# First projection stage: the feed-forward product is rounded to 16-bit steps by ScalarE, and its scale moves into the residual addition

## The chip, the cores and the metric

The kernel runs on one core of one Trainium2 chip. The metric is the device time of one execution in microseconds (us), less is better.

## The reference, cut to what matters

The program turns 32 images and texts (NB = 32 samples of T = 273 tokens, D = 256 channels) into tokens, then runs two transformer layers. The part around the change is the end of the first layer's feed-forward block and the entry of the second layer's attention:

```python
def act_qdq(x):                       # 16-bit quantise and dequantise, one scale for the whole tensor
    scale = max(max(abs(x)) / 32767, 1e-12)
    return clip(round(x / scale), -32768, 32767) * scale
o = act_qdq(gate * up)                          # [32, 273, 768]
h = h + o @ lpbq_dequant(w_down).T              # down projection, residual
x = layernorm(h)
q, k, v = split(x @ qkv_w.T)                    # then rotary embedding, norms of some heads
```

## The kernel before

The program is a row of stages, each over all 32 samples. The changed one is `phase_f1`, the first projection stage. It takes about 740 of 5506 us, from 1262 to 2000 us of the trace. For each sample it loads the product `o` (128 partitions x 6 x 273 numbers, f32) and the residual `h`, and does this:

- `round_o` (L1121, ScalarE): `om = o * inv + MAGIC`, which rounds to whole steps in f32.
- `quantise_o` (L1185, VectorE): `o = (om - MAGIC) * scale`, in place.
- `down` (L1277, TensorE): 36 matmuls of 256 columns into PSUM banks 0 and 1.
- `residual` (L1191 and L1193, VectorE): adds PSUM to `h`, in two instructions of 512 and 256 elements. Then come the layer norm's statistics (L98, L102).
- `normalise` (L109, VectorE), `turn_x` (L128, TensorE, transposes), `copy_x` (L1127, ScalarE).
- `project` (L1292 and L1302, TensorE): 12 matmuls of 512 columns for queries and keys into banks 4 to 6, 12 of 256 for the values. `values_and_squares` (L1132, L1135, L1145, ScalarE) copies the values out.
- `rotate` (L1214 to L1228, VectorE), `norms` (L1150, ScalarE), `scale_heads` (L1233 to L1240, VectorE).
- `turn_heads` (L1320, TensorE): turns queries and keys through banks 2, 3 and 1. `upper_parts` (L1157, L1166, ScalarE) and `lower_parts` (L1249, L1258, VectorE) split each turned tile into three bf16 parts, which SP stores.

Everything has two buffers (`u` = sample number modulo 2). Each engine runs its functions in a fixed order, written out by hand: `pipeline` calls, in each turn b, every listed function for sample b plus its lead. Semaphores order the engines; an instruction that waits holds back all that stand behind it on its engine. The orders before are

```python
pipeline(act, NB, ((copy_x, 0), (round_o, 2), (upper_parts, -1), (values_and_squares, 0), (norms, 0)))
pipeline(dve, NB, ((scale_heads, -1), (quantise_o, 2), (residual, 1), (lower_parts, -1), (normalise, 1),
                   (rotate, 0)))
pipeline(pe, NB, ((turn_x, 0), (down, 1), (turn_heads, -1), (project, 0)))
```

So VectorE does `scale_heads` of sample b-1, then `quantise_o` of sample b+2, then `residual` of sample b+1. `down` of b+1 is followed on TensorE by `turn_heads` of b-1, which waits for that residual, because bank 1 holds both the last third of the down product and a turned tile:

```python
if not isinstance(n[0], int) or 2 * n[0] + n[1] + 2 < NB:
    pe.wait_ge(S["h2"].sem, S["h2"].at((n[0], n[1] + 2)))
```

Of the kernel before, what the change touches and what calls it, by code (L numbers as in the profile page):

```python
# [7 lines left out]
ALU = mybir.AluOpType  # L8
ACT = mybir.ActivationFunctionType
AX = mybir.AxisListType  # L10

D = 256
CT = D // 128
PATCHES, TEXT = 196, 77
T = T_BATCH = PATCHES + TEXT
R = 91
NT = T // R
# [3 lines left out]
FT = FF // 128  # L21
# [5 lines left out]
MAGIC = 12582912.0  # L27
# [28 lines left out]
def signals(ctx, nc, prefix, **pers):  # L56
    return {k: Signal(nc, f"{prefix}_{k}", per, skew) for skew, (k, per) in enumerate(pers.items())}
# [80 lines left out]
def phase_a(nc, c, ps, NB, patches_dram, txt_dram, wtok_dram, wq_dram, wk_dram, wv_dram, wo_dram,  # L138
# [4 lines left out]
    with ctx:  # L143
# [3 lines left out]
        def sem(name):  # L147
            return nc.alloc_semaphore("a_" + name)
# [30 lines left out]
        passed = sem("passed")  # L179
        S = signals(ctx, nc, "a", tok=1, tok_out=1, bn=NT + 1, mv=1, eps=1, rstd=1, xn=NT, xT=1, xT_out=1,  # L180
                    g=1, g_out=1, v=1, v_out=1, s=NT, mx=NT, nb=1, p=NT, pT=1, pT_out=1, rden=1, y=1, h1=1,
# [15 lines left out]
        def _(sp):  # L197
# [7 lines left out]
            def next_patches(n, u, i):  # L205
                if following(n, NB):
                    sp.wait_ge(S["tok"].sem, S["tok"].at(n))
                    sp.sem_inc(passed, 1)
                    load_patches((n[0], n[1] + 2), u)

            def store_h1(n, u, i):
                sp.wait_ge(S["h1"].sem, S["h1"].at(n))
                sp.sem_inc(passed, 1)
# [6 lines left out]
            def store_x0(n, u, i):  # L220
                sp.wait_ge(S["x0T_out"].sem, S["x0T_out"].at(n))
                sp.sem_inc(passed, 1)
                sp.dma_start(x0_dram[batch_of(n)].rearrange("(c p) t -> p c t", p=128), x0T[:, u])\
                    .then_inc(x0_stored[u], 16)
# [15 lines left out]
        def _(pool):  # L240
            for k in ("eps", "rstd", "eps1", "rstd1"):
                S[k].give(pool)

            def deviation_h(n, u, i):
                ln_rstd(nc, pool, c, mv[:, u], var_eps[:, u], rstd[:, u], S["mv"], S["eps"], S["rstd"], n)

# [345 lines left out]
def back(n, by):  # L592

    return (n[0], n[1] - by)
# [353 lines left out]
def pipeline(eng, NB, stages):  # L948

    def turn(i, b):
        for stage, lead in stages:
            k = b + lead
            if not isinstance(i, int) or 0 <= 2 * i + k < NB:
                stage((i, k), k % 2, i + k // 2)

    for b in range(-3, 2):
        turn(0, b)
    with eng.Fori(1, NB // 2 - 2) as i:  # L960
        for b in range(2):
            turn(i, b)
    for b in range(5 + NB % 2):
        turn(NB // 2 - 2, b)
# [7 lines left out]
def following(n, NB):  # L972

    return not isinstance(n[0], int) or 2 * n[0] + n[1] + 2 < NB
# [7 lines left out]
def phase_f1(nc, c, ps, NB, magic, o_dram, h1_dram, downT, scale, inv, wqkv_dram, curv_dram,  # L982
# [3 lines left out]
    ctx = ExitStack()  # L986
    with ctx:
        def sb(name, shape, dt=F32):
            return ctx.enter_context(nc.sbuf_tensor("f_" + name, shape, dt))

        def sem(name):
            return nc.alloc_semaphore("f_" + name)
# [8 lines left out]
        wqkv = sb("wqkv", [128, CT, 3 * D])  # L1001
        icurv = sb("icurv", [R, 4])
        o = sb("o", [128, 2, FT, T])
        om = sb("om", [128, 2, FT, T])
        h = sb("h", [R, 2, NT, D])
        stats = sb("stats", [R, 2, NT, 6])
        mv = sb("mv", [R, 2, NT, 2])
        var_eps = sb("var_eps", [R, 2, NT])
        rstd = sb("rstd", [R, 2, NT])
        xn = sb("xn", [R, 2, NT, D])  # L1010
        xT = sb("xT", [128, 2, CT, T])
        rc = sb("rc", [R, 2, 2, HD, H])
# [3 lines left out]
        sq = sb("sq", [R, 2, 2, HD, NSCALED])  # L1016
        ss = sb("ss", [R, 2, NT * 2, NSCALED])
        norm = sb("norm", [R, 2, NT * 2, NSCALED])
        parts = sb("parts", [128, 2, NTILE, PARTS, T], BF16)
        rest = sb("rest", [128, 2, 2, T])  # L1020
# [6 lines left out]
        h_stored = [sem(f"h_stored{u}") for u in range(2)]  # L1027
        p_stored = [sem(f"p_stored{u}") for u in range(2)]
        v_stored = [sem(f"v_stored{u}") for u in range(2)]
        S = signals(ctx, nc, "f", om=1, oq=1, y=1, h2=1, bn=NT + 1, mv=1, eps=1, rstd=1, xn=NT, xT=1, xT_out=1,  # L1030
                    qk=NT, v=2, v_out=2, rc=2 * NT, rot=NT, sq=NT, ss=NT, cap=2, norm=1, inv=1, tq=2, scaled=NT,
                    turn=NTILE, hi=NTILE, rest=NTILE, mid=NTILE, lo=NTILE)
        block = ctx.enter_context(nc.Block())
# [78 lines left out]

        @block.scalar
        def _(act):
            for k in ("om", "xT_out", "v_out", "sq", "norm", "hi", "mid"):
                S[k].give(act)

            def round_o(n, u, i):
                act.wait_ge(o_loaded[u], 16 * (i + 1))
                act.wait_ge(S["oq"].sem, S["oq"].before(n))  # L1120
                nc.scalar.activation(om[:, u], o[:, u], ACT.Identity, scale=inv, bias=magic)\  # L1121
                    .then_inc(S["om"].sem, 1)

            def copy_x(n, u, i):
                act.wait_ge(S["xT"].sem, S["xT"].at(n))
                act.wait_ge(S["v"].sem, S["v"].before(n))
                nc.scalar.copy(xT[:, u], ps[:, 2:4, 0:T]).then_inc(S["xT_out"].sem, 1)  # L1127

            def values_and_squares(n, u, i):
                act.wait_ge(v_stored[u], 16 * i)  # L1130
                act.wait_ge(S["v"].sem, S["v"].at(n, 1))
                nc.scalar.copy(vp[:, u, 0:2, :, 0:HD], ps[0:R, 7, :].rearrange("p (t h w) -> p t h w", t=2, w=HD))\  # L1132
                    .then_inc(S["v_out"].sem, 1)
                act.wait_ge(S["v"].sem, S["v"].at(n, 2))
                nc.scalar.copy(vp[:, u, 2, :, 0:HD], ps[0:R, 0, 0:D].rearrange("p (h w) -> p h w", w=HD))\  # L1135
                    .then_inc(S["v_out"].sem, 1)
                for t in range(NT):
                    act.wait_ge(S["rot"].sem, S["rot"].at(n, t + 1))

                    if t:  # L1140
                        act.wait_ge(S["ss"].sem, S["ss"].at(n, t))
                    else:
                        act.wait_ge(S["ss"].sem, S["ss"].before(n))
                    heads = qk[:, u, t, :, :, 6:16]
                    nc.scalar.activation(sq[:, u], heads, ACT.Square).then_inc(S["sq"].sem, 1)  # L1145

            def norms(n, u, i):
                act.wait_ge(S["cap"].sem, S["cap"].at(n))
                act.wait_ge(S["scaled"].sem, S["scaled"].before(n))
                nc.scalar.activation(norm[:, u], ss[:, u], ACT.Sqrt).then_inc(S["norm"].sem, 1)  # L1150

            def upper_parts(n, u, i):
                act.wait_ge(p_stored[u], STORES * i)
                for j in range(NTILE):
                    rows = ROWS[j]
                    act.wait_ge(S["turn"].sem, S["turn"].at(n, j + 1))
                    nc.scalar.copy(parts[0:rows, u, j, part_place(TILES[j][0], 0), :],  # L1157
                                   ps[0:rows, TURN[j % 3], 0:T]).then_inc(S["hi"].sem, 1)
                    if j:
                        second_part(n, u, j - 1)  # L1160
                second_part(n, u, NTILE - 1)

            def second_part(n, u, j):
                rows = ROWS[j]
                act.wait_ge(S["rest"].sem, S["rest"].at(n, j + 1))
                nc.scalar.copy(parts[0:rows, u, j, 1, :], rest[0:rows, u, j % 2]).then_inc(S["mid"].sem, 1)  # L1166

            pipeline(act, NB, ((copy_x, 0), (round_o, 2), (upper_parts, -1), (values_and_squares, 0), (norms, 0)))

        @block.vector  # L1170
        def _(dve):
            for k in ("oq", "h2", "bn", "mv", "xn", "rc", "rot", "ss", "inv", "tq", "scaled", "rest", "lo"):
                S[k].give(dve)
            dve.wait_ge(w_loaded, 32)
            nc.vector.reciprocal(icurv[:], icurv[:]).then_inc(filled, 1)
# [4 lines left out]
            nc.vector.memset(vp[:], 1.0).then_inc(filled, 1)  # L1180
            dve.wait_ge(filled, 3)

            def quantise_o(n, u, i):
                dve.wait_ge(S["om"].sem, S["om"].at(n))
                nc.vector.tensor_scalar(o[:, u], om[:, u], MAGIC, scale, ALU.subtract, ALU.mult)\  # L1185
                    .then_inc(S["oq"].sem, 1)

            def residual(n, u, i):
                dve.wait_ge(S["y"].sem, S["y"].at(n))
                dve.wait_ge(h_loaded[u], 16 * (i + 1))  # L1190
                nc.vector.tensor_tensor(h[:, u, 0:2, :], ps[0:R, 0, :].rearrange("p (t d) -> p t d", t=2),  # L1191
                                        h[:, u, 0:2, :], ALU.add)
                nc.vector.tensor_tensor(h[:, u, 2, :], ps[0:R, 1, 0:D], h[:, u, 2, :], ALU.add)\  # L1193
                    .then_inc(S["h2"].sem, 1)
                dve.wait_ge(S["h2"].sem, S["h2"].at(n))
                dve.wait_ge(S["xn"].sem, S["xn"].before(n))
                ln_stats(nc, dve, h[:, u], stats[:, u], mv[:, u], (S["bn"].sem, S["bn"].at(n)), S["mv"])
# [57 lines left out]
            def third_part(n, u, j):  # L1255
# [2 lines left out]
                nc.vector.tensor_tensor(parts[0:rows, u, j, part_place(TILES[j][0], 2), :], rest[0:rows, u, j % 2],  # L1258
                                        parts[0:rows, u, j, 1, :], ALU.subtract).then_inc(S["lo"].sem, 1)

            pipeline(dve, NB, ((scale_heads, -1), (quantise_o, 2), (residual, 1), (lower_parts, -1), (normalise, 1),
                               (rotate, 0)))

        @block.tensor
# [1266 lines left out]
```

## Time and profile before

| | |
|---|---|
| median of 3 runs | 5524.6 us (5519.47 to 5539.08) |
| profiled execution | 5507.82 us, its span 5506.1 us |
| TensorE busy | 4410.9 us (80%) |
| VectorE busy | 3717.9 us (68%) |
| ScalarE busy | 2374.3 us (43%) |
| GpSimd busy | 599.8 us (11%) |
| mean granted TensorE clock | 0.867 of full speed |

The span is the time from the first to the last instruction on the core. Shares of busy time are means over stages with different limits, so they do not say what bounds the changed stage. PE is TensorE, PEld its weight load, DVE VectorE, ACT ScalarE, POOL GpSimd, SPq the queue of SyncE. In the rows below a timeline row gives start, length, engine, line and operation, output and inputs, count, and in brackets the idle time of the engine ahead of it with what ended it. A row of the windows view gives the stretch and its length, then the busy time of PE, PEld, DVE, ACT and POOL with the number of instructions, then the granted TensorE clock, the share of the DMA engines and GB/s. A row of the groups view gives line, engine, operation, names, shapes and count, then the busy time in us, the mean ns of one, and the idle time before them.

### The profile page before, as it was taken

What the parts mean: (1) busy time and instruction counts of PE and PEld (TensorE: products, weight loads), DVE (VectorE), ACT (ScalarE), POOL (GpSimd) and SP (SyncE); (2) the same over time, 40 slices, a digit from 0 to 9 for tenths busy, and PEclk for the clock granted to TensorE, in tenths of its full rate; (3) what the DMA queues carried; (4) which work ended last, traced back from release to release, by engine and by line L of the source; (5) the groups of instructions that cost most, each with busy time, mean ns of one, the idle gap of its engine ahead of it and who ended that gap; (6) DMA issues with size and microseconds to landing.
All of it is one profiled execution on the core that took longest, in us unless ns stands there. A gap on an engine that the chain in (4) does not pass through costs nothing. (4 is left out here: it accounts for less than half of the span.)

```text
span 5506.1 us, 99275 instructions
## 1 busy us (share of the span) xinstructions
PE 4410.9 (80%) x26575; PEld 2865.4 (52%) x26575; DVE 3717.9 (68%) x9205; ACT 2374.3 (43%) x5474; POOL 599.8 (11%) x928
## 2 busy tenths in 40 slices
PE   6999788506888857777777767776998999688898
PEld 5777666303555535555555545554555555344444
DVE  4555439766777867766666645556777777477776
ACT  1222237552333337677767732223666666100000
POOL 0111000000000010000000011111111111122221
PEclk8999999857999977777777778888999999899999
DMA  2222369994444432222222235554333333211110
GB/s 80 76 73 76 125 232 385 372 418 146 129 123 129 131 81 69 69 75 71 66 69 75 69 86 155 155 156 105 93 92 92 92 89 75 68 52 46 49 46 26
DMA packets 389665, 635.48 MB, mean 115 GB/s; under 512 B 44598, under 2 KB 311412, under 8 KB 389492
## 3 DMA queue, kind: packets, MB, share of 16 engines
q1 hardware_dynamic: 377172, 632.25, 37.9%
q0 software_dynamic: 12320, 1.40, 0.2%
q8 instruction: 50, 0.82, 0.1%
q14 instruction: 123, 1.01, 0.1%
HBM read 353.96 MB, written 278.15 MB: 115 GB/s over the span
## 5 line engine op out<-in xcount | busy, mean ns | idle before, releaser
L1729 DVE TENSOR_REDUCE e_neg<-ps 91x1 f32<-91x273 f32 x1536 | 571.9, 427 | 136.2 <-PE ps L1550 128.8
L1662 ACT ACTIVATE e_probT<-ps 91x273 f32<-91x273 f32 x1536 | 491.5, 392 | 290.2 <-PE ps L1550 289.6
L2404 PE MATMUL ps<-m_we,m_xT 128*128 128x512 f32 x1104 | 524.2, 624 | 0.0
L1277 PE MATMUL ps<-k_downT,f_o 128*91 128x256 f32 x1152 | 260.1, 385 | 230.3 <-DVE f_o L1185 230.2
L1548 PE MATMUL ps<-c_mask_kq,c_identb 91*91 91x91 bf16 x1536 | 325.9, 243 | 110.7 <-ACT g_probT L1662 81.1
L1550 PE MATMUL ps<-e_k,e_q 96*91 96x273 bf16 x1536 | 343.5, 305 | 62.1 <-DMA e_k<-s_parts 27.3
L2338 DVE SCALAR_TENSOR_TENSOR m_acc<-ps,m_weight,m_acc 128x256 f32<-128x256 f32 x552 | 261.8, 481 | 178.9 <-PE ps L2404 168.4
L1550 PE MATMUL ps<-g_q,g_k 102*91 102x273 bf16 (+5 forms) x1536 | 329.4, 295 | 49.7 <-DVEq L1735 48.2
L1277 PEld LDWEIGHTS ps<-k_downT,f_o 128*91 128x91 f32 x1152 | 182.9, 161 | 299.1 <-issue 231.3
L2404 PEld LDWEIGHTS ps<-m_we,m_xT 128*128 128x128 f32 x1104 | 212.5, 199 | 224.7 <-issue 212.2
L1550 PE MATMUL ps<-e_q,e_k 128*91 128x273 bf16 x1536 | 285.6, 290 | 38.5 <-DMA e_q<-e_shift 36.6
L1548 PEld LDWEIGHTS ps<-c_mask_kq,c_identb 91*91 91x91 bf16 x1536 | 217.8, 152 | 182.5 <-ACT g_probT L1662 139.1
L1550 PEld LDWEIGHTS ps<-e_k,e_q 96*91 96x91 bf16 x1536 | 173.6, 123 | 246.8 <-DVE e_neg L1729 194.6
L1662 ACT ACTIVATE g_probT<-ps 91x273 f32<-91x273 f32 x768 | 263.7, 388 | 51.4 <-PE ps L1550 47.4
L1548 PE MATMUL ps<-c_mask_qk,c_identb 91*91 91x91 bf16 x960 | 216.5, 252 | 79.2 <-DVE g_neg L1729 39.6
L1619 PE MATMUL ps<-g_probT,g_vp 128*32 128x273 f32 (+2 forms) x3072 | 256.2, 415 | 23.9 <-ACT g_probT L1662 23.9
L1619 PE MATMUL ps<-e_probT,e_vp 128*32 128x273 f32 x3072 | 258.9, 409 | 8.8 <-ACT e_probT L1662 6.1
L1550 PEld LDWEIGHTS ps<-g_q,g_k 102*91 102x91 bf16 (+1 forms) x1536 | 219.2, 151 | 86.7 <-DVEq L1735 80.7
L1533 POOL DMA_DIRECT2D e_q<-e_shift x288 | 144.5, 508 | 767.4 <-DVE e_shift L1771 761.5
L1550 PEld LDWEIGHTS ps<-e_q,e_k 128*91 128x91 bf16 x1536 | 176.0, 124 | 96.5 <-issue 37.2
L606 PE MATMUL ps<-c_x,k_upT 128*128 128x273 f32 x768 | 186.9, 400 | 47.1 <-DMA c_x<-s_xq 47.1
L1550 PE MATMUL ps<-g_k,g_q 102*91 102x273 bf16 (+2 forms) x960 | 221.1, 302 | 0.0
(306 smaller groups left out, 9435.6 us busy)
## 6 DMA issues: line engine op xcount, KB each, us to landing
s_gate<-b_gate SPq DMA_DIRECT2D x32, 819.0 KB
c_g<-s_gate SPq DMA_DIRECT2D x32, 819.0 KB, 11.7
s_up<-c_up SPq DMA_DIRECT2D x32, 819.0 KB
s_gated<-c_gated SPq DMA_DIRECT2D x32, 819.0 KB
d_g<-s_gated SPq DMA_DIRECT2D x32, 819.0 KB, 10.0
d_u<-s_up SPq DMA_DIRECT2D x32, 819.0 KB, 10.3
s_o<-d_o SPq DMA_DIRECT2D x32, 819.0 KB
f_o<-s_o SPq DMA_DIRECT2D x32, 819.0 KB, 4.6
```

The lines of the kernel that those rows point to most:

```text
L606: last = nc.tensor.matmul(ps[:, f, 0:T], w[:, k, f * 128:(f + 1) * 128], x[:, k, :], start=(k == 0), stop=(k == CT - 1))
L1277: last = nc.tensor.matmul(ps[0:R, t // 2, (t % 2) * D:(t % 2 + 1) * D], o[:, u, k, t * R:(t + 1) * R], downT[:, k, :], start=(k == 0), sto ...
L1533: pool.dma_start(q[rows + part:rows + part + 1, u, lo:hi, :], shift[0:hi - lo, u, part, :]).then_inc(laid[u], 16)
L1548: nc.tensor.matmul(ps[0:R, bank, col + col_of_mask:col + col_of_mask + R], c["identb"][0:R, 0:R], c[mask][0:R, 0:R], start=True, stop=Fals ...
L1550: return nc.tensor.matmul(out_, stationary, moving, start=mask is None, stop=True, skip_group_check=mask is not None)
L1619: last = nc.tensor.matmul(ps[32 * a:32 * a + VW, 6, q0:T], vp[:, u, kt, ORDER[j], :], probT[:, j % 8, b, col:col + T - q0], start=(kt == 0 ...
L1662: nc.scalar.activation(probT[0:R, p % 8, b, :], src, ACT.Exp, scale=float(HD) ** 0.5 if kinds[h] == COS else 1.0)\
L1729: last = nc.vector.tensor_reduce(neg[:, u, t, h:h + 1], src, AX.X, ALU.max, negate=True)
L2338: nc.vector.scalar_tensor_tensor(out=acc[:, u, t], in0=ps[0:R, EBANK[m % 4], j * D:(j + 1) * D], scalar=weight[:, u, t, 2 * p + j:2 * p + ...
L2404: last = nc.tensor.matmul(ps[0:R, EBANK[m % 4], :], xT[:, u, k, t * R:(t + 1) * R], we[:, k, 2 * p:2 * p + 2, :].rearrange("p e d -> p (e ...
```

## The change

ScalarE's rounding pass writes whole steps as int16 into a new buffer `steps` (the conversion rounds) in place of `om`. A second ScalarE pass, `restore_o`, behind `upper_parts`, copies the steps back into `o` as f32, without the scale. VectorE's `quantise_o` is gone. The down projection so yields the product divided by `scale`, and `residual` multiplies by `scale` while it adds (`scalar_tensor_tensor` with a per-partition scalar in place of `tensor_tensor`).

```diff
-        om = sb("om", [128, 2, FT, T])
+        steps = sb("steps", [128, 2, FT, T], mybir.dt.int16)
...
             def round_o(n, u, i):
                 act.wait_ge(o_loaded[u], 16 * (i + 1))
-                act.wait_ge(S["oq"].sem, S["oq"].before(n))
-                nc.scalar.activation(om[:, u], o[:, u], ACT.Identity, scale=inv, bias=magic)\
-                    .then_inc(S["om"].sem, 1)
+                act.wait_ge(S["oq"].sem, S["oq"].at(back(n, 2)))
+                nc.scalar.activation(steps[:, u], o[:, u], ACT.Identity, scale=inv).then_inc(S["steps"].sem, 1)
+
+            def restore_o(n, u, i):
+                act.wait_ge(S["steps"].sem, S["steps"].at(n))
+                nc.scalar.copy(o[:, u], steps[:, u]).then_inc(S["oq"].sem, 1)
...
-            pipeline(act, NB, ((copy_x, 0), (round_o, 2), (upper_parts, -1), (values_and_squares, 0), (norms, 0)))
+            pipeline(act, NB, ((copy_x, 0), (round_o, 2), (upper_parts, -1), (restore_o, 2), (values_and_squares, 0), (norms, 0)))
...
-            def quantise_o(n, u, i):
-                dve.wait_ge(S["om"].sem, S["om"].at(n))
-                nc.vector.tensor_scalar(o[:, u], om[:, u], MAGIC, scale, ALU.subtract, ALU.mult)\
-                    .then_inc(S["oq"].sem, 1)
-
             def residual(n, u, i):
...
-                nc.vector.tensor_tensor(h[:, u, 0:2, :], ps[0:R, 0, :].rearrange("p (t d) -> p t d", t=2),
-                                        h[:, u, 0:2, :], ALU.add)
-                nc.vector.tensor_tensor(h[:, u, 2, :], ps[0:R, 1, 0:D], h[:, u, 2, :], ALU.add)\
+                nc.vector.scalar_tensor_tensor(out=h[:, u, 0:2, :], in0=ps[0:R, 0, :].rearrange("p (t d) -> p t d", t=2),
+                                               scalar=scale[0:R], in1=h[:, u, 0:2, :], op0=ALU.mult, op1=ALU.add)
+                nc.vector.scalar_tensor_tensor(out=h[:, u, 2, :], in0=ps[0:R, 1, 0:D], scalar=scale[0:R],
+                                               in1=h[:, u, 2, :], op0=ALU.mult, op1=ALU.add)\
                     .then_inc(S["h2"].sem, 1)
...
-            pipeline(dve, NB, ((scale_heads, -1), (quantise_o, 2), (residual, 1), (lower_parts, -1), (normalise, 1),
+            pipeline(dve, NB, ((scale_heads, -1), (residual, 1), (lower_parts, -1), (normalise, 1),
                                (rotate, 0)))
```

## Rows read from the trace of the kernel before

**Rows 1.** Windows view: 27 samples together, then four samples one after another.
```profile
1320.98:1918.81 597.83, 534.01 (x2187) 325.33 (x2188) 479.33 (x1162) 223.83 (x486) 42.39 (x108) 0.90 0.44 126
1608.77:1630.10 21.33, 17.88 (x81) 11.17 (x82) 17.66 (x43) 8.21 (x18) 1.57 (x4) 1.00 0.50 148
1630.10:1652.57 22.47, 20.90 (x82) 12.76 (x82) 17.84 (x43) 8.41 (x18) 1.57 (x4) 0.85 0.38 111
1652.57:1675.74 23.17, 20.90 (x81) 12.35 (x81) 17.83 (x43) 8.21 (x18) 1.57 (x4) 0.85 0.45 122
1675.74:1697.52 21.78, 19.51 (x82) 11.88 (x82) 17.72 (x43) 8.31 (x18) 1.57 (x4) 0.92 0.43 130
```
**Rows 2.** Windows view: the start of the second of these samples.
```profile
1630.20:1636.90 6.70, 6.34 (x20) 3.54 (x21) 6.17 (x19) 3.63 (x10) 1.07 (x2) 0.50 0.69 216
```
**Rows 3.** Timeline from the down projection to the turned heads that follow it.
```profile
1619.72 8.01 PE L1277 MATMUL ps<-k_downT,f_o 128*91 128x256 f32 x36
...
1626.26 1.75 ACT L1121 ACTIVATE f_om<-f_o,k_magic,k_inv_o 128x1638 f32<-128x1638 f32 x1
1626.29 0.89 DVE L1240 TENSOR_TENSOR f_qk<-f_qk,f_norm 91x192 f32<-91x192 f32 x3
...
1628.05 1.07 DVE L1185 TENSOR_SCALAR f_o<-f_om,k_scale_o 128x1638 f32<-128x1638 f32 x1 [0.87 <-ACT f_om L1121]
1629.03 0.68 DVE L1191 TENSOR_TENSOR f_h<-ps,f_h 91x512 f32<-91x512 f32 x1
...
1630.10 1.63 PE L1320 MATMUL ps<-c_ident,f_qk 91*128 91x91 f32 x9 [2.38 <-DVE f_h L1193]
...
1633.05 7.25 PE L1292 MATMUL ps<-f_wqkv,f_xT 128*91 128x512 f32 x12
```
**Rows 4.** Timeline, the same place one sample earlier.
```profile
1608.77 0.93 PE L1320 MATMUL ps<-c_ident,f_qk 91*128 91x91 f32 x9 [1.21 <-DVE f_h L1193]
...
1611.35 5.32 PE L1292 MATMUL ps<-f_wqkv,f_xT 128*91 128x512 f32 x12
```
**Rows 5.** Timeline, the same place one sample later.
```profile
1650.31 1.07 DVE L1185 TENSOR_SCALAR f_o<-f_om,k_scale_o 128x1638 f32<-128x1638 f32 x1 [1.19 <-ACT f_om L1121]
...
1652.57 0.92 PE L1320 MATMUL ps<-c_ident,f_qk 91*128 91x91 f32 x9 [1.21 <-DVE f_h L1193]
```
**Rows 6.** ScalarE around the new pass: timeline, then its wait over the 27 samples.
```profile
1613.80 0.42 ACT L1166 CAST f_parts<-f_rest 8x273 bf16<-8x273 f32 x1 [0.39 <-DVE f_rest L1249]
...
1618.43 0.58 ACT L1132 COPY f_vp<-ps 91x512 f32<-91x512 f32 x1 [4.21 <-PE ps L1302]
...
  PE ps L1302: 159.2, 27
```
**Rows 7.** Groups view by form, ScalarE.
```profile
L1121 ACT ACTIVATE f_om<-f_o,k_magic,k_inv_o 128x1638 f32<-128x1638 f32 x32 | 56.1, 1754 | 24.1 <-DMA f_o<-s_o 24.1
...
L791 ACT ACTIVATE c_sig<-c_steps,k_scale_gate 128x1638 f32<-128x1638 int16 x32 | 53.2, 1664 | 0.0
...
L904 ACT ACTIVATE d_gs<-d_g,k_inv_gated 128x1638 int16<-128x1638 f32 x32 | 53.1, 1660 | 89.7 <-DMA d_g<-s_gated 47.8 <-DVE d_o L920 41.9
...
L1127 ACT COPY f_xT<-ps 128x546 f32<-128x546 f32 x32 | 19.5, 610 | 16.3 <-PE ps L128 13.6 <-issue 2.8
```
**Rows 8.** Groups view by form, VectorE.
```profile
L351 DVE SCALAR_TENSOR_TENSOR a_h<-ps,a_rden,a_h 98x256 f32<-98x256 f32 x64 | 28.0, 480 | 97.4 <-PE ps L467 97.4
...
L1191 DVE TENSOR_TENSOR f_h<-ps,f_h 91x512 f32<-91x512 f32 x32 | 21.9, 685 | 16.1 <-PE ps L1277 15.3
...
L1193 DVE TENSOR_TENSOR f_h<-ps,f_h 91x256 f32<-91x256 f32 x32 | 13.1, 410 | 0.0
```
**Rows 9.** Timeline, the stage's first samples.
```profile
1275.10 9.68 PE L1277 MATMUL ps<-k_downT,f_o 128*91 128x256 f32 x36 [230.21 <-DVE f_o L1185]
...
1317.09 0.89 DVE L1240 TENSOR_TENSOR f_qk<-f_qk,f_norm 91x192 f32<-91x192 f32 x3
...
1319.83 0.68 DVE L1191 TENSOR_TENSOR f_h<-ps,f_h 91x512 f32<-91x512 f32 x1
```

More of the change, by code:

```diff
@@ L1029, in phase_f1 @@
         v_stored = [sem(f"v_stored{u}") for u in range(2)]
-        S = signals(ctx, nc, "f", om=1, oq=1, y=1, h2=1, bn=NT + 1, mv=1, eps=1, rstd=1, xn=NT, xT=1, xT_out=1,
+        S = signals(ctx, nc, "f", steps=1, oq=1, y=1, h2=1, bn=NT + 1, mv=1, eps=1, rstd=1, xn=NT, xT=1, xT_out=1,
                     qk=NT, v=2, v_out=2, rc=2 * NT, rot=NT, sq=NT, ss=NT, cap=2, norm=1, inv=1, tq=2, scaled=NT,
@@ L1114, in _ @@
         def _(act):
-            for k in ("om", "xT_out", "v_out", "sq", "norm", "hi", "mid"):
+            for k in ("steps", "oq", "xT_out", "v_out", "sq", "norm", "hi", "mid"):
                 S[k].give(act)
@@ L1166, in second_part @@
                 nc.scalar.copy(parts[0:rows, u, j, 1, :], rest[0:rows, u, j % 2]).then_inc(S["mid"].sem, 1)
-            pipeline(act, NB, ((copy_x, 0), (round_o, 2), (upper_parts, -1), (values_and_squares, 0), (norms, 0)))
+            pipeline(act, NB, ((copy_x, 0), (round_o, 2), (upper_parts, -1), (restore_o, 2), (values_and_squares, 0), (norms, 0)))
         @block.vector
         def _(dve):
-            for k in ("oq", "h2", "bn", "mv", "xn", "rc", "rot", "ss", "inv", "tq", "scaled", "rest", "lo"):
+            for k in ("h2", "bn", "mv", "xn", "rc", "rot", "ss", "inv", "tq", "scaled", "rest", "lo"):
                 S[k].give(dve)
```

## The prediction

> **What bounds the stage.** I read the windows view first, cut at the instants at which TensorE starts the turned heads. The stage goes in a steady step: 27 samples take 597.83 us, 22.14 each [rows 1]. TensorE is busy for 534 of them and VectorE for 479, so neither is full, and the question is which wait ends last. The four single samples differ: 21.33, 22.47, 23.17 and 21.78 us, 22.19 on average, and their granted clock differs with them: 1.00, 0.85, 0.85, 0.92. I call them A, B, C and D; the mean over 27 samples says that this group of four stands for the loop.
>
> The timeline shows the two things that lengthen them. First a gap on TensorE. The down projection ends at 1619.72 + 8.01 = 1627.73, and the turned heads behind it start at 1630.10, 2.38 us later, released by the residual [rows 3]. One sample earlier and one later the same gap is 1.21 us [rows 4, 5]. The reader is to see why: VectorE has finished the head scaling at 1626.29 + 0.89 = 1627.18, before the down projection ends, but the next thing in its order is the quantise pass, which waits for ScalarE's rounding (1626.26 + 1.75 = 1628.01) and ends at about 1629.1. Only then does the residual start, at 1629.03. In [rows 5] the quantise pass starts at 1650.31 and is over just as the down projection ends, so there it delays nothing. So one gap in four is 1.17 us too long, and in the other three the residual itself is the 1.21 us.
>
> Second, the clock. After the long gap the granted clock is 0.50, that is 1.2 in place of 2.4 GHz, over 6.70 us [rows 2], and the 12 projection matmuls take 7.25 us [rows 3] against 5.32 at full clock [rows 4]. What the engine did before it fell: it stood idle for 2.38 us. But C and D have low stretches too, and ahead of these stood gaps of only 1.21 us, as ahead of A, which has none. So a gap of 1.21 us is enough at some places and not at others.
>
> Without a fall and without a late residual a sample takes 21.33 - 1.17 = 20.16 us (A less the excess of the gap at its end). Measured against that, the clock costs 0 in A, 22.47 - 20.16 = 2.31 in B, 3.01 in C and 1.62 in D: 1.73 a sample on average. The excess gap is 0.29 a sample. 20.16 + 0.29 + 1.73 = 22.18, which closes against [rows 1].
>
> **The change, part by part.**
>
> *VectorE loses the quantise pass*: 32 x 1.07 us [rows 3], and the residual loses the wait for ScalarE that stood in its way. The head scaling is over 0.55 us before the down projection ends, so in an A the residual will start when TensorE releases it. Every gap then is the short one: -0.29 us a sample. Next late behind the residual is the residual itself, which nothing in this change shortens.
>
> *The residual's two instructions become multiply-and-add* with a scalar read from each partition. The nearest row, with PSUM, scalar and SBUF operand in the same places, takes 480 ns for 256 elements, and the addition of 256 that it replaces takes 410 [rows 8]. I charge 0.07 us once for this and 0.06 for the 512-element one (685 now): +0.13 us a sample. It lies on the path, in the gap. Bounds: 0, if the extra time is hidden in the overlap of two neighbours, and 0.14, both in full.
>
> *ScalarE's rounding pass* loses the bias and writes int16. The nearest row with just these operands is 1660 ns against 1754 now [rows 7]: 0.09 us less. It stands between 1626.26 and 1628.01 and the turned heads, the next to need ScalarE, come after, so I count nothing.
>
> *ScalarE gains the restoring pass*, int16 to f32, 1638 elements. The trace does not have a plain copy of that size. Its nearest row, an activation from int16 to f32 of the same shape, takes 1.66 us; three copies of 546 elements would be 1.83 as an upper bound, and VectorE's pass of 1.07 a lower one [rows 3, 7]. I take 1.66. What hides it: ScalarE ends the casts at 1613.80 + 0.42 = 1614.22 and idles 4.21 us for the value matmuls, and over 27 samples that wait adds up to 159.2 us, 5.9 each [rows 6]. 1614.22 + 1.66 = 1615.9 leaves 2.5 us in a sample at full clock. The values' copy, the squares and the norms stand behind it on ScalarE, and TensorE's next down projection behind the values' copy. If the cover were gone, all 1.66 would be on the path. The down projection needs the restored `o` one turn later, at 1619.72, 3.8 us after it is ready. No DMA is added or moved, and the load of the next `o` still waits for the down projection alone, so SP's queue keeps its order.
>
> A rule speaks against this part. The Trainium skill, "ScalarE: Activation LUTs", section "Rules for kernel authors", says to give plain adds and multiplications to VectorE and not to ScalarE, since VectorE is the faster one there. The rows agree on the price (1.66 against 1.07 us), and by that rule the move would add about 0.6 us to each of 32 samples, some 19 us, where the work was not hidden; here the idle stretch of ScalarE decides. The same page, "What ACT_TABLE_LOAD costs", gives 186 ns + 0.833 ns an element for an activation with constant scale and bias; my estimate from it is 1.55 us for the restoring pass, which would leave the sum as it is.
>
> *The clock.* This is the large term and the trace of before does not hold it: every gap will be 1.21 + 0.13 = 1.34 us and none 2.38. Bounds: at best the clock holds in all samples, as in A (0). At worst each sample loses what C loses (3.01). Between them I look at the samples that had the short gap ahead: A, C and D lose 0, 3.01 and 1.62, on average 1.54. But C and D always come one and two samples after the long gap of B, and an A comes as soon as that is past, so I take the long gap as what throws the rhythm off, and falls as rarer without it. They will not vanish, since a gap of 1.21 us has been seen to be enough. I take half of that average, 0.77 us a sample. This is a choice and no row proves it.
>
> *The start.* The first down projection waits for the quantised `o` with nothing to cover it [rows 9]: 1.66 in place of 1.07, +0.59 us once. The first residual in the loop starts at 1319.83, though the head scaling was over at 1317.98 and the down projection earlier: -1.85 once. Together -1.3.
>
> **Sum.** A sample: 20.16 + 0.13 + 0.77 = 21.06 us, in place of 22.14: -1.08. 27 of them make -29.2, the start -1.3: -30.5 us. The profiled execution (5507.8 us, 1.7 of it outside the span) would go to 5477. It was faster than all three runs shown; from their median of 5524.6 the same step gives 5494 us, 0.55% less.
>
> **Rivals.**
> - *The clock holds throughout.* A sample of 20.29 us: 27 x 1.85 + 1.3 = 51 us less, 5473. For it: A. Against it: C and D.
> - *The clock falls as before.* Its loss stays between 1.54 and 1.73: 27 x 0.31 + 1.3 = 9.7, or 27 x 0.12 + 1.3 = 4.5 us less: 5515 to 5520. For it: two of three short gaps now are followed by a fall.
> - *The clock falls in each sample* (slower). The place is the gap ahead of the turned heads, now of one length and so perhaps locked to the clock's rhythm at a bad spot. The price is C's: 20.29 + 3.01 = 23.30, 27 x 1.16 - 1.3 = 30 us more, 5555. It decides from a mean loss of 1.90 us. For it: C. Against it: two C never stand side by side.
> - *ScalarE becomes the late one.* The restoring pass sits in front of the values' copy; it decides once the casts end 2.5 us later than now. At full price 27 x (1.66 - 1.08) - 1.3 = 14 us more, 5539. Against it: 5.9 us of mean idle time.
>
> **How the numbers follow.** Only about 0.5%, 27.6 us, can be told from no change. My forecast gets 0.60, with a range of its own from 5487 to 5501 (a clock loss of 0.5 to 1.0 us a sample); a good two thirds of it, 0.43, lie beyond 0.5%. The holding clock gets 0.12, all faster; the old clock 0.17, all same; the bad lock 0.06, of which 0.05 slower; late ScalarE 0.05, of which 0.01 slower. Faster 0.55, same 0.39, slower 0.06. The range goes from the holding clock to the old one, 5472 to 5520, and leaves out the two slower cases and the ends.
>
> **What would show it right or wrong.** Right: no gap near 2.4 us ahead of the turned heads, all at 1.3; a residual pair longer by 0.13 us; the two ScalarE passes near 1.66 us each, and 2.5 us or more still idle ahead of the values' copy; the loop near 21.1 us a sample, its granted clock up from 0.90 to about 0.95. Wrong: gaps that are gone while the clock stays at 0.90 (the old clock), a clock near 0.85 in every sample (the bad lock), or TensorE's down projection waiting for ScalarE.

## The result and the profile after

The changed kernel takes 5494.56 us (median of 6 runs, 5478.89 to 5510.71) where the kernel before, timed beside it, takes 5530.7. The ratio is 0.9936, 95% interval 0.991 to 0.9961: 0.64% faster. The forecast was 5494 us and 0.55%. The profiled execution took 5478.89 us with a span of 5477.2; against the profiled execution before, the span is 28.9 us shorter, where the sum had said 30.5.

The windows view of the changed kernel, first 27 samples from turned heads to turned heads, then four single samples, then 23 samples that start behind the first three. It answers to [rows 1].

```profile
1324.52:1897.03 572.51, 508.42 (x2188) 312.21 (x2188) 453.91 (x1135) 259.94 (x513) 42.43 (x108) 0.95 0.46 133
1604.09:1624.37 20.28, 17.89 (x82) 11.17 (x82) 16.79 (x42) 9.58 (x19) 1.58 (x4) 1.00 0.45 139
1624.37:1644.64 20.27, 17.87 (x81) 11.16 (x81) 16.79 (x42) 9.67 (x19) 1.57 (x4) 1.00 0.49 140
1685.19:1708.45 23.26, 20.86 (x81) 12.31 (x82) 16.87 (x42) 9.57 (x19) 1.57 (x4) 0.85 0.40 122
1708.45:1730.34 21.89, 19.49 (x82) 11.91 (x82) 16.80 (x42) 9.67 (x19) 1.57 (x4) 0.92 0.43 129
1392.36:1876.74 484.38, 429.24 (x1863) 264.23 (x1864) 386.54 (x966) 221.29 (x437) 36.15 (x92) 0.96 0.46 134
```

The loop goes from 22.14 to 572.51 / 27 = 21.20 us a sample and its granted clock from 0.90 to 0.95. A sample without a fall of the clock is 20.28 us; C and D of before are still there (23.26 and 21.89), but now they come as a pair after three or four samples at full clock, and B with its long gap is gone. In all, 11 of the 27 samples hold a fall, against 20 before.

The timeline of one sample, from VectorE's head scaling to the turned heads and on to the values' copy, answers to [rows 3, 4, 6]:

```profile
1621.57 1.66 ACT L1121 ACTIVATE f_steps<-f_o,k_inv_o 128x1638 int16<-128x1638 f32 x1
1621.60 0.89 DVE L1239 TENSOR_TENSOR f_qk<-f_qk,f_norm 91x192 f32<-91x192 f32 x3
1623.17 0.75 DVE L1189 SCALAR_TENSOR_TENSOR f_h<-ps,k_scale_o,f_h 91x512 f32<-91x512 f32 x1 [0.69 <-PE ps L1276]
...
1624.37 0.92 PE L1319 MATMUL ps<-c_ident,f_qk 91*128 91x91 f32 x9 [1.33 <-DVE f_h L1191]
...
1626.35 0.45 PE L1319 MATMUL ps<-c_ident,f_qk 91*128 91x91 f32 x3 [1.06 <-DVE f_rest L1248]
...
1629.71 1.55 ACT L1125 CAST f_o<-f_steps 128x1638 f32<-128x1638 int16 x1
```

The residual now waits for TensorE (0.69 us of idle VectorE in front of it) and not for ScalarE's rounding. The gap ahead of the turned heads is 1.33 us here, and 1.33 or 1.34 in every sample of the loop but the first (1.97); before, one gap in four was 2.37 or 2.38.

Where the low clock sets in shows in the sample of 23.26 us, and likewise in C of before (the last row):

```profile
1685.19 0.92 PE L1319 MATMUL ps<-c_ident,f_qk 91*128 91x91 f32 x9 [1.34 <-DVE f_h L1191]
1687.19 0.72 PE L1319 MATMUL ps<-c_ident,f_qk 91*128 91x91 f32 x3 [1.07 <-DVE f_rest L1248]
...
1654.56 0.71 PE L1320 MATMUL ps<-c_ident,f_qk 91*128 91x91 f32 x3 [1.07 <-DVE f_rest L1249]
```

The first nine turned matmuls still run as fast as at full clock (0.92 us). The next three, behind TensorE's second wait, of 1.07 us, take 0.72 us where they take 0.45 at full clock. So two idle times stand close together ahead of such a fall, and the prediction names only the first.

The groups view, of the stage, answers to [rows 7, 8]:

```profile
L1121 ACT ACTIVATE f_steps<-f_o,k_inv_o 128x1638 int16<-128x1638 f32 x32 | 53.2, 1662 | 22.3 <-DMA f_o<-s_o 22.3
L1125 ACT CAST f_o<-f_steps 128x1638 f32<-128x1638 int16 x32 | 49.7, 1552 | 0.1
...
L1189 DVE SCALAR_TENSOR_TENSOR f_h<-ps,k_scale_o,f_h 91x512 f32<-91x512 f32 x32 | 23.9, 747 | 61.1 <-PE ps L1276 61.0
L1191 DVE SCALAR_TENSOR_TENSOR f_h<-ps,k_scale_o,f_h 91x256 f32<-91x256 f32 x32 | 15.1, 471 | 0.0
```

### The profile page after: what moved, and what is told of

Its sections match the earlier page's. It is cut to its first block and busy times, and to the rows that moved or that the text cites. A ratio compares the mean times of both kernels' runs of the same rounds, so it can differ in the third digit from the quotient of the medians.

```text
span 5477.2 us, 99287 instructions
## 1 busy us (share of the span) xinstructions
PE 4378.4 (80%) x26575; PEld 2848.0 (52%) x26575; DVE 3686.6 (67%) x9173; ACT 2417.8 (44%) x5506; POOL 599.3 (11%) x928
```

## The experiments

All edits are to `phase_f1` and all numbers a sample are means over the same 27 samples, from turned heads to turned heads (from residual to residual in the last two). The loop is the measure, since whole executions of one kernel differ by 10 us and more. Of the profiled executions, one for each kernel, the stages outside the changed one (ahead of its first rounding and behind its last turned heads) take between 4778 and 4801 us, though nothing in them was edited. What the whole times say stands behind the last run. The theory is that of the prediction: a residual that comes late lengthens TensorE's gap, and the gaps make the clock fall in some samples. The rivals are named with each run.

**The order alone.** The kernel before, with nothing moved to ScalarE; only VectorE's order is changed.

```diff
-            pipeline(dve, NB, ((scale_heads, -1), (quantise_o, 2), (residual, 1), (lower_parts, -1), (normalise, 1),
+            pipeline(dve, NB, ((scale_heads, -1), (residual, 1), (lower_parts, -1), (quantise_o, 2), (normalise, 1),
```

> The kernel before with one edit: VectorE keeps its quantise pass, but runs it behind the lower parts, no longer in front of the residual. Theory (the late residual sets off falls of the clock): no gap of 2.4 us is left; VectorE's own chain grows by 1.07 us past the residual, so a sample without a fall is near 20.6 us, and the loop's mean falls from 22.14 to between 20.7 and 21.7 us, most of what the change gave (21.20). Rival (the gain is VectorE's lighter load): VectorE is as busy as before, 17.7 us a sample, so the loop stays near 22.1 us.

Windows view of its loop, then the longest gap in it behind the first sample:

```profile
1324.21:1896.70 572.49, 507.99 (x2188) 312.28 (x2188) 475.77 (x1162) 222.92 (x486) 42.23 (x108) 0.95 0.46 133
...
1599.34 0.93 PE L1320 MATMUL ps<-c_ident,f_qk 91*128 91x91 f32 x9 [1.49 <-DVE f_h L1193]
```

21.20 us a sample, the same as the changed kernel to 0.02 us in 572, with VectorE as busy (475.77 us) as before the change (479.33 in [rows 1]) and not at 453.91. The gaps ahead of the turned heads are 1.21 to 1.49 us. The rival falls: it is not VectorE's lighter load that gave the loop's gain. Samples without a fall are 20.36 to 20.43 us, for VectorE's chain is now the later one by a little, and the pairs of falls come a little more rarely. The time is 0.9958 of before (0.9931 to 0.9986).

**A shorter gap.** The changed kernel, its scale multiplied once into the down weights, the residual a plain addition.

```diff
+            nc.vector.tensor_scalar(downT[:], downT[:], scale, None, ALU.mult).then_inc(filled, 1)
...
-                nc.vector.scalar_tensor_tensor(out=h[:, u, 0:2, :], in0=ps[0:R, 0, :].rearrange("p (t d) -> p t d", t=2),
-                                               scalar=scale[0:R], in1=h[:, u, 0:2, :], op0=ALU.mult, op1=ALU.add)
+                nc.vector.tensor_tensor(h[:, u, 0:2, :], ps[0:R, 0, :].rearrange("p (t d) -> p t d", t=2),
+                                        h[:, u, 0:2, :], ALU.add)
```

> The changed kernel, with the scale multiplied once into the down projection's weights at the stage's start, so that the residual is the plain addition again. Both theories: the gap ahead of the turned heads goes from 1.34 to 1.21 us. Rival (the gap's length is what counts): every sample is 0.13 us shorter, the loop's mean goes from 21.20 to 21.07 us. Theory (it counts where a gap falls against the rhythm of the clock): a sample without a fall is 20.15 us, but falls come more often, one pair in four samples, and the mean is 21.1 to 21.4 us, not faster than 21.20.

**A longer gap.** The changed kernel, its residual in three instructions.

```diff
+                for t in range(NT):
+                    last = nc.vector.scalar_tensor_tensor(out=h[:, u, t, :], in0=ps[0:R, t // 2, (t % 2) * D:(t % 2 + 1) * D],
+                                                          scalar=scale[0:R], in1=h[:, u, t, :], op0=ALU.mult, op1=ALU.add)
```

> The changed kernel, with the residual in three instructions of 256 elements in place of one of 512 and one of 256: 0.11 us more in the gap, 1.45 us. Rival (the gap's length counts): 21.20 + 0.11 = 21.31 us a sample. Theory (rhythm): a sample without a fall is 20.39 us, the pairs of falls come more rarely, and the mean is 20.6 to 20.9 us, though the gap is longer; with a chance of one in ten the rhythm locks in a bad place and it is above 22.

Windows view of the loop with the shorter gap, and one of its gaps:

```profile
1321.07:1892.80 571.73, 510.48 (x2188) 312.84 (x2188) 450.59 (x1135) 259.90 (x513) 42.41 (x108) 0.95 0.46 133
...
1620.06 0.92 PE L1319 MATMUL ps<-c_ident,f_qk 91*128 91x91 f32 x9 [1.21 <-DVE f_h L1192]
```

Windows view of the loop with the longer gap:

```profile
1328.68:1886.46 557.78, 489.82 (x2187) 304.38 (x2188) 456.99 (x1162) 259.88 (x513) 42.40 (x108) 0.98 0.46 137
```

Timeline of the latter, two turns of heads:

```profile
1614.12 0.92 PE L1318 MATMUL ps<-c_ident,f_qk 91*128 91x91 f32 x9 [1.45 <-DVE f_h L1190]
...
1634.52 0.92 PE L1318 MATMUL ps<-c_ident,f_qk 91*128 91x91 f32 x9 [1.46 <-DVE f_h L1190]
```

The shorter gap gives 571.73 / 27 = 21.18 us a sample, no gain to speak of though each sample without a fall went to 20.15; the falls ate it. The longer gap gives 20.66, with samples of 20.40 and only one pair of falls and the first half of a second in 27 samples (granted clock 0.98). So in its profile the loop became 0.54 us a sample faster while the gap that it waits for became longer by 0.12. The rival, that only the length of the gap counts, had 21.07 and 21.31; both loops refute it. The whole times do not show this difference: timed side by side, the two kernels have medians of 5484.66 us (shorter gap, 12 runs) and 5483.84 us (longer, 11 runs), where the loops are 14 us apart. In the two profiled executions the stages outside took 16 us more with the longer gap. Whether its loop is as fast in other executions is not shown.

**The gap filled.** The changed kernel with added work: matmuls whose result nobody reads, ahead of the wait for the residual.

```diff
+                    for _ in range(5):
+                        nc.tensor.matmul(ps[:, TURN[0], 0:D], wqkv[:, 0, 0:128], wqkv[:, 0, 0:D], start=True, stop=True)
                     pe.wait_ge(S["h2"].sem, S["h2"].at((n[0], n[1] + 2)))
```

> The changed kernel with added work: ahead of its wait for the residual TensorE runs five matmuls of 256 columns (1.08 us at full clock) whose result nobody reads. Theory (the idle time ahead of the turned heads lets the clock fall): idle time there goes from 1.34 to about 0.25 us, the granted clock is 1.00 through the loop, every sample takes 20.3 us, 0.9 less than 21.20. Rival (the falls come from something else, such as the turned heads themselves or the later wait of 1.07 us): the falls stay and the mean stays at 21.2 us or goes up.

Timeline of TensorE in one of its samples, then the windows view of the loop:

```profile
1590.59 8.01 PE L1276 MATMUL ps<-k_downT,f_o 128*91 128x256 f32 x36
1598.43 2.32 PE L1314 MATMUL ps<-f_wqkv 128*128 128x256 f32 x10
1600.59 0.87 PE L1322 MATMUL ps<-c_ident,f_qk 91*128 91x91 f32 x9
1602.01 0.46 PE L1322 MATMUL ps<-c_ident,f_qk 91*128 91x91 f32 x3 [0.54 <-DVE f_rest L1248]
```

```profile
1315.61:1864.97 549.36, 535.41 (x2458) 354.88 (x2457) 454.81 (x1134) 259.84 (x513) 42.38 (x108) 1.00 0.47 138
```

Each of the five calls is two matmul instructions in f32, so the filling is twice what the expectation says: ten, 2.16 us from the first to the turned heads. It fills the whole gap and makes the turned heads later by 0.66 us, counted from the down projection's end; the idle time behind the first nine of them shrinks from 1.06 to 0.54. The clock is 1.00 through the loop and nearly every sample takes 20.30 to 20.38 us (the first 20.68), 549.36 / 27 = 20.35 on average: 0.86 a sample, 23 us in all, less than the changed kernel, with more work. The turned heads are all still there, so it is the idle time around them that lets the clock fall, and not they themselves. Which of the two idle times it is, this run does not separate, since the filling shortens both.

**The gap filled in the kernel before.** The same edit there, the late quantise pass kept.

> The kernel before, with the same five added matmuls of 256 columns, unread, ahead of TensorE's wait for the residual; VectorE's order and work as before. Theory (two prices, the clock's 1.73 us and the late residual's 0.29 us a sample): the clock holds, and then the quantise pass is late in every sample, so each takes what A takes, 21.33 us, 0.8 less than 22.14 and 1.0 more than the filled kernel after (20.35). Rival (the late residual costs only through the clock): with the clock held the sample goes to 20.3 us here too.

Windows view of its loop, then VectorE's timeline in one sample, then TensorE's behind it:

```profile
1319.66:1904.52 584.86, 550.13 (x2457) 356.07 (x2457) 478.31 (x1162) 222.79 (x486) 42.23 (x108) 0.98 0.47 130
```

```profile
1599.05 1.07 DVE L1185 TENSOR_SCALAR f_o<-f_om,k_scale_o 128x1638 f32<-128x1638 f32 x1 [1.19 <-ACT f_om L1121]
1600.04 0.68 DVE L1191 TENSOR_TENSOR f_h<-ps,f_h 91x512 f32<-91x512 f32 x1
...
1601.11 0.93 PE L1323 MATMUL ps<-c_ident,f_qk 91*128 91x91 f32 x9 [0.60 <-DVE f_h L1193]
1603.10 0.46 PE L1323 MATMUL ps<-c_ident,f_qk 91*128 91x91 f32 x3 [1.07 <-DVE f_rest L1249]
```

584.86 / 27 = 21.66 us, 0.48 less than before and 0.33 above the calculation, because some idle time is still left behind the filling and the clock still falls at places (0.98): in 6 samples of 27, where 20 had a fall before. Most samples at full clock take 21.31 to 21.33 and 21.70 or 21.71 us in turn, and counted from residual to residual no sample is under 21.3: the late residual then costs its 1 us in nearly every sample. The run also bears on the two idle times. In 21 of the samples the second wait is as long as ever (0.97 to 1.07 us) while the first is only 0.21 to 0.64; six of these hold a fall and 15 do not. So the second wait with so short a first one is mostly not enough for a fall. The rival's 20.3 falls. So the two prices of the prediction, 0.29 and 1.73 us, do not simply add: in the kernel before, the three gaps behind the fall in B are short, for a slow TensorE gave VectorE the time to catch up, and so a fall hid the next late residual.

**The restoring pass twice.** The changed kernel, with a second copy of the steps into a buffer that nobody reads.

```diff
+                act.wait_ge(S["again"].sem, S["again"].before(n))
+                nc.scalar.copy(again[:], steps[:, u]).then_inc(S["again"].sem, 1)
```

> The changed kernel, with the restoring pass done a second time into a buffer that nobody reads: 1.55 us more on ScalarE in each sample. Theory (ScalarE's wait for the value matmuls hides the pass, 2.6 us being left in a sample without a fall): the loop stays at 21.2 us a sample, and ScalarE's wait ahead of the values' copy shrinks by 1.55 us. Rival (the pass is partly on the path): up to 1.55 us more, 22.7.

Windows view of its loop, then ScalarE's wait for the value matmuls over the 27 samples, in the changed kernel and here:

```profile
1320.33:1892.76 572.43, 508.38 (x2188) 312.25 (x2188) 453.90 (x1135) 299.17 (x540) 42.24 (x108) 0.95 0.48 133
...
  PE ps L1301: 99.4, 27
...
  PE ps L1304: 59.9, 27
```

ScalarE is busy for 299.17 us in place of 259.94, and the loop is the same, 21.20. ScalarE's wait goes from 99.4 to 59.9 us. The pass is hidden, and a second would be.

**The turned heads earlier.** The changed kernel; the wait for the residual moves to the third turned tile, which is the one that needs bank 1, and VectorE does two remainders ahead of the statistics.

```diff
-                if not isinstance(n[0], int) or 2 * n[0] + n[1] + 2 < NB:
-                    pe.wait_ge(S["h2"].sem, S["h2"].at((n[0], n[1] + 2)))
                 for j, (a, d0) in enumerate(TILES):
+                    if j == 2 and (not isinstance(n[0], int) or 2 * n[0] + n[1] + 2 < NB):
+                        pe.wait_ge(S["h2"].sem, S["h2"].at((n[0], n[1] + 2)))
...
-            pipeline(dve, NB, ((scale_heads, -1), (residual, 1), (lower_parts, -1), (normalise, 1),
+            pipeline(dve, NB, ((scale_heads, -1), (residual, 1), (lower_first, -1), (statistics, 1), (lower_rest, -1), (normalise, 1),
```

> The changed kernel, with the wait for the residual moved from the first to the third turned tile, the only one that shares a bank with the down product, and on VectorE the first two remainders moved ahead of the layer norm's statistics, so that the fourth tile's wait ends earlier. Theory: TensorE's two idle times of 1.34 and 1.07 us shrink by about 1.5 us together, then VectorE's chain from one residual to the next (19.5 us) sets the step: 19.5 us a sample without a fall, 19.5 to 20.7 on average with falls. Rival (the two waits hang on the same chain and merely change places): 20.3 us without a fall, 21.2 on average, as now.

**The same, with scale in the weights and filling.** Four calls of the filling (eight matmuls) ahead of the third tile's wait, and the scale in the down weights.

> The kernel of the run before it, with the scale in the down weights and four added unread matmuls ahead of the third turned tile's wait. Theory: VectorE's chain of 19.4 us sets the step and the clock holds, so 19.4 us a sample, 1.8 less than 21.20, and some 50 us less in the whole than the changed kernel. Rival (the added matmuls are late themselves, since they can run only behind two turned tiles): TensorE is the late one again, near 20.3 us.

Windows view of the loop of the first of the two:

```profile
1326.30:1857.62 531.32, 498.31 (x2190) 307.50 (x2191) 448.64 (x1136) 258.62 (x514) 47.24 (x108) 0.98 0.47 144
```

VectorE's timeline in the same kernel, a residual that starts as soon as the head scaling is over:

```profile
1621.11 0.89 DVE L1241 TENSOR_TENSOR f_qk<-f_qk,f_norm 91x192 f32<-91x192 f32 x3
1621.92 0.74 DVE L1189 SCALAR_TENSOR_TENSOR f_h<-ps,k_scale_o,f_h 91x512 f32<-91x512 f32 x1
```

Windows view of the loop of the second:

```profile
1324.87:1849.94 525.07, 522.70 (x2404) 341.34 (x2405) 446.94 (x1135) 260.27 (x514) 47.22 (x108) 1.00 0.52 145
```

The first takes 531.32 / 27 = 19.68 us a sample; VectorE now is the later one in most samples, as its residual follows the head scaling with no idle time. The run moves the wait and changes VectorE's order together, so the share of each is not shown. The second takes 19.45 at a clock of 1.00, as forecast from VectorE's chain, and is TensorE's to keep too, for it is busy for 522.70 of 525.07 us. Its time is 5442.25 us, 0.9836 of the kernel before (0.9815 to 0.9858), the fastest of all. The first is at 0.9869 (0.9842 to 0.9897).

**The whole times.** Time against the kernel before timed beside it, with its 95% interval:

| kernel | loop, us a sample | time against before |
|---|---|---|
| changed | 21.20 | 0.9936 (0.991 to 0.9961) |
| order alone | 21.20 | 0.9958 (0.9931 to 0.9986) |
| shorter gap | 21.18 | 0.9937 (0.9915 to 0.9958) |
| longer gap | 20.66 | 0.993 (0.9908 to 0.9952) |
| gap filled | 20.35 | 0.9922 (0.9898 to 0.9945) |
| gap filled, before | 21.66 | 0.9964 (0.9946 to 0.9983) |
| restoring twice | 21.20 | 0.9937 (0.9912 to 0.9962) |
| heads earlier | 19.68 | 0.9869 (0.9842 to 0.9897) |
| the same, filled | 19.45 | 0.9836 (0.9815 to 0.9858) |

All are faster than before, but the intervals of the first five overlap, so what sets these apart rests on the loops, one profile each. The order alone is the one to doubt: timed side by side with the two runs on the gap's length, which are variants of the changed kernel, it has a median of 5499.61 us against their 5484.66 and 5483.84, though its loop is as short as that of the first of them. Where these 15 us lie is open.

## Why the prediction was right, point by point

- *The late residual is gone.* Right, as the gaps show. The step was also right on what replaces the wait: VectorE stands ready 0.6 to 0.7 us before TensorE in a sample without a fall, and over 2 us before it in one with a fall.
- *The price of the multiply-and-add.* Forecast +0.13 us; the two instructions went from 685 and 410 to 747 and 471 ns and the gap from 1.21 to 1.33 or 1.34. A sample without a fall was put at 20.29 us and takes 20.28.
- *The clock.* Forecast a loss of 0.77 us a sample, in place of 1.73; measured 21.20 - 20.28 = 0.92 over the 27 samples, and 484.38 / 23 - 20.28 = 0.78 behind the first three. This was called a choice, and its size was luck in part: the run with the shorter gap shows a loss of 21.18 - 20.15 = 1.03, that with the longer one 0.26. The argument behind it, that without the long gap falls become rarer, holds: a pair of falls now comes after three or four full samples. The argument that the long gap alone throws the rhythm off does not hold as put, for C and D come without any B. The list of what TensorE did ahead of the falls in C and D, a gap of 1.21 us, was short by the second wait of 1.07 us, behind which the low clock shows.
- *ScalarE.* The rounding takes 1.66 us as forecast. The restoring pass takes 1.55 and not 1.66, which changes nothing, since it is hidden; the doubled pass shows that directly. The estimate from the Trainium skill, "ScalarE: Activation LUTs", section "What ACT_TABLE_LOAD costs", had been 1.55, and the trace agrees. The Trainium skill's rule in "Rules for kernel authors" of the same page, which spoke against the move, is true of the price (1.55 against 1.07 us) and did not decide the time here: the pass stands in an idle stretch.
- *The start.* Forecast -1.3 us. From the first rounding to the first down projection takes 0.3 us more (3.35 against 3.04) and from there to the third residual 1.3 less: -1.0.
- *The sum.* 27 samples gave 25.3 us in place of 29.2. From the first rounding to the last turned heads the stage is 725.8 us before and 699.4 after, 26.4 less; the other 2.5 of the span's 28.9 us lie in stages that the change does not touch, and the 35 us that the ratio stands for lie a little above both, inside its interval. That the median hit the forecast of 5494 us to 1 us is luck: the loop gave 3.9 us less than forecast, and the six executions lie 32 us apart.
- *The rivals.* The clock that falls as before, that in each sample, and the late ScalarE did not come. The holding clock is what the filled kernel reaches by other means.

What the forecast did not see is that moving the work to ScalarE was not needed for the loop: the order alone gives the same one. That it gives the same whole time is not shown.

## What to carry to other kernels

Where one pass stands in front of a more urgent one in an engine's fixed order, first try to move it behind; that costs a line and gave here the same loop as moving it to another engine. Idle time of TensorE was paid twice here, as itself and in the clock, and the second part depends on where it falls: judge a change to such a gap over many samples, and test by filling the gap with unread matmuls. When a wait is due to a shared bank, put it at the first instruction that touches that bank and not ahead of the group.

## What the runs showed of the hardware that was not expected

In one profile each, gaps of 1.21, 1.33 and 1.45 us ahead of the turned heads went with loops of 21.18, 21.20 and 20.66 us a sample, while samples without a fall grew from 20.15 to 20.28 and 20.40; the whole times of the first and the last do not differ, so that a longer gap makes the program faster is not shown. Ten unread matmuls a sample made the loop 20.35. On ScalarE one pass over 1638 elements took 1754 ns with a scale and a bias read per partition (f32 to f32), 1662 with the scale alone (f32 to int16) and 1552 with neither (int16 to f32); with the scale alone from int16 to f32 it took 1664 [rows 7].
